# All 86 pacing waits removed from GpSimd's gathers in a field-interaction kernel with a two-layer top

## The reference, cut to what matters

```python
e = stack([tbl_f[ids[:, f]] for f in range(32)], axis=1)      # (512, 32, 16)
x = e
for W in (W0, W1, W2):                                        # (32, 32 or 64, 64)
    x = relu(einsum('bmd,bhd,mhk->bkd', e, x, W))             # e times x for all pairs (m, h)
    outs.append(x.sum(axis=2))                                # 64 features a layer
h = concat([concat(outs, 1), dense_ctx], 1)
h = relu(h @ W_top1 + b_top1); h = relu(h @ W_top2 + b_top2); y = h @ W_top3
```

## Time and profile before

| | |
|---|---|
| median of 3 runs | 333.96 us (333.34 to 334.33) |
| profiled execution | 333.23 us, of which the span from the first to the last instruction is 331.4 us |
| TensorE busy | 303.6 us of the span |
| VectorE busy | 267.0 us |
| GpSimd busy | 244.0 us, 121.8 of it 128 gathers, 121.4 of it 53 products |
| mean granted TensorE clock | 0.99 |

### The profile page before, as it was taken

One profiled execution on the slowest core, in us unless ns is written; L12 is line 12 of the kernel. 1 busy time (PEld: TensorE's weight loads), 2 busy tenths in 40 slices (PEclk: granted clock), 3 DMA queues, 4 the chain that ended last, 5 costly groups with the idle time before them and its releaser, 6 DMA issues.

```text
span 331.4 us, 4576 instructions
## 1 busy us (share of the span) xinstructions
PE 303.6 (92%) x1760; PEld 131.7 (40%) x1760; DVE 267.0 (81%) x162; ACT 65.3 (20%) x105; POOL 244.0 (74%) x187
## 2 busy tenths in 40 slices
PE   0469899999869989999999899999999999999996
PEld 0335535654436233333333233344434434434334
DVE  0118399676978999999999999999899999999110
ACT  1030511435000130122122101032213032020011
POOL 5677777778888789999888799999686539966000
PEclk9997999999989999999999999999999999999999
DMA  6364848771388869687679489929979995230000
GB/s 189 95 195 138 242 107 238 206 211 21 87 267 285 292 227 297 230 269 244 203 233 318 141 251 322 323 98 266 385 316 320 313 292 130 60 85 1 0 2 0
DMA packets 32220, 65.43 MB, mean 197 GB/s; under 512 B 5702, under 2 KB 12870, under 8 KB 32198
## 3 DMA queue, kind: packets, MB, share of 16 engines
q1 hardware_dynamic: 20614, 52.28, 46.8%
q10 hardware_dynamic: 7488, 11.80, 12.3%
q0 software_dynamic: 4096, 1.06, 3.9%
HBM read 51.35 MB, written 1.71 MB: 160 GB/s over the span
## 4 chain that ended last, share of the span: by engine, by line
PE 63%; DVE 10%; issue 9%; POOL 4%; ACT 1%; ACTq 0%; DVEq 0%; POOLq 0%
PE acc L956 55%; DVE vz L746 9%; POOL gathered L674 3%; PE factor L1001 2%; PE factor L996 1%; POOL pz L691 1%; PE acc L969 1%; PE factor L911 1%; PE acc L951 1%; PE factor L926 1%; PE factor L1008 1%; DVE feats L756 1%; PE acc L1001 1%; ACT factor L792 0%; ACTq L869 0%
## 5 line engine op out<-in xcount | busy, mean ns | idle before, releaser
L746 DVE TENSOR_TENSOR vz<-fields_sb,factor 128x1024 f32<-128x1024 f32 (+3 forms) x113 | 229.0, 2076 | 32.2 <-PE factor L911 11.1
L956 PE MATMUL acc<-vz,w_sb 128*64 128x512 f32 (+1 forms) x1020 | 197.8, 525 | 6.4 <-DVE vz L746 6.0
L674 POOL DMA_INDIRECT gathered<-in_table,index x128 | 121.8, 952 | 38.1 <-issue 31.0
L691 POOL TENSOR_TENSOR pz<-fields_sb,hidden 128x1024 f32<-128x1024 f32 (+1 forms) x53 | 121.4, 2314 | 19.0 <-DMA hidden<-relu_out 15.0
L956 PEld LDWEIGHTS acc<-vz,w_sb 128*64 128x64 f32 x1020 | 78.6, 139 | 111.3 <-issue 84.1
L956 PE MATMUL acc<-pz,w_sb 128*64 128x512 f32 (+1 forms) x212 | 52.9, 583 | 2.7 <-POOL pz L691 2.7
L858 ACT ACTIVATE relu_out<-acc 128x512 f32<-128x512 f32 (+1 forms) x30 | 15.4, 514 | 111.2 <-PE acc L956 85.8
L792 ACT ACTIVATE factor<-hidden 128x1024 f32<-128x1024 f32 (+1 forms) x26 | 23.6, 914 | 64.5 <-DMA hidden<-relu_out 45.0
L956 PEld LDWEIGHTS acc<-pz,w_sb 128*64 128x64 f32 x212 | 17.1, 137 | 30.1 <-issue 25.7
L746 DVE TENSOR_TENSOR vz<-rotated,factor 128x2048 f32<-128x2048 f32 x10 | 22.4, 2279 | 0.0
L756 DVE TENSOR_REDUCE feats<-relu_out 128x32 f32<-128x512 f32 (+1 forms) x30 | 17.1, 570 | 6.4 <-ACT relu_out L858 6.4
(11 more groups left out here) (35 smaller groups left out, 52.6 us busy)
## 6 DMA issues: line engine op xcount, KB each, us to landing
fields_sb<-fields SPq DMA_DIRECT2D x48, 512.0 KB, 5.0
rotated<-fields SPq DMA_DIRECT2D x20, 512.0 KB, 6.4
hidden<-relu_out ACTq DMA_DIRECT2D x38, 256.0 KB, 5.7
fields_sb<-fields SPq DMA_DIRECT2D x32, 256.0 KB, 3.3
own<-fields SPq DMA_DIRECT2D x5, 512.0 KB, 5.9
gathered<-in_table,index POOLq DMA_INDIRECT x128, 4.1
hidden<-relu_out ACTq DMA_DIRECT2D x14, 128.0 KB, 3.9
fields<-gathered SPq DMA_DIRECT2D x5, 256.0 KB, 2.2
```

The lines of the kernel that those rows point to most:

```text
L674: nc.gpsimd.indirect_dma_start(gathered[:, pair % GRING, j, :], None, table, bass.IndirectOffsetOnAxis(ap=index[:, i:i + 1], axis=0)).then ...
L691: nc.gpsimd.tensor_tensor(pz[:, at % PRING, 0:cols], fields[s][:, t, col:col + cols], hidden_of(step, g), ALU.mult).then_inc(pz_ready, 1)
L746: nc.vector.tensor_tensor(vz[:, at:at + nt, 0:cols].rearrange("p t (a n) -> p t a n", n=half), src[:, t:t + nt, col:col + cols].rearrange( ...
L956: last = nc.tensor.matmul(acc_of(step, ab), weights[:, kt, :], z[:, ab * half:(ab + 1) * half], start=start and j == 0, stop=stop and j == ...
```

## The change

Three tables are emptied, nothing else is changed. Gather 8 no longer waits for gather 7's landing, no gather waits for a count of TensorE's units, and none for the first spread. The order of instructions on every engine, the gathers themselves and the waits for a free place in the ring `gathered` stay.

```diff
-PACED = {12: 1, 14: 1, 15: 1, 16: 1, 17: 1, 19: 1, 20: 1, 22: 1, 24: 1, 25: 1, 26: 1, 32: 1, 34: 1, 35: 1, 36:
...
-    48, 117: 49, 118: 49, 119: 49, 120: 52, 121: 56, 123: 68, 124: 74, 125: 75, 126: 79}
-
-
-BEHIND_SPREAD = {15: 1, 41: 1, 59: 1, 75: 1, 81: 1}
-
-AFTER_ROW = (8,)
+PACED = {}
+
+
+BEHIND_SPREAD = {}
+
+AFTER_ROW = ()
```

## The result

The changed kernel takes 331.41 us in the median of six runs (331.36 to 331.55). The kernel before takes 333.21 us: six runs, 332.87 to 334.33, the three that the forecast had and three more beside the changed kernel (332.87, 332.95 and 333.09). The medians differ by 1.8 us, 0.54%. The ratio of all runs is 0.9935, 95% interval 0.9918 to 0.9951, which is a gain of 1.6 to 2.7 us. Forecast were 332.1 us, a gain of 1.9 us, the forecast's own range of 331.7 to 332.6 us and the 8-in-10 range of 331.1 to 333.8 us.

A forecast was written before the change was run, and what follows sets the result against it. GpSimd's lateness was taken to bound it, through TensorE's stall at 97 us with no slack behind. 0 + 1.35 + 0.42 + 0.1 = 1.9 us off 333.96 gave 332.1 us; own range 331.7 to 332.6, 8-in-10 range 331.1 to 333.8.

The forecast's parts named there:

- the base of the sum: Starting time of the forecast: 333.96 us, the median of the runs before, 0.73 us above its profiled execution of 333.23.
- 84 passed waits at nothing: On GpSimd's gathers: removing 84 waits that had passed already gains 0 us, 0.8 us at most.
- Gather 8 and gather 15, 1.77 us: GpSimd's gaps ahead of these gathers shrink to 0.30 us: 1.35 and 0.42 us, together 1.77 us earlier.
- The head at 0.1 to 0.2 us: At the start, descriptors of gathers 8 and 9 share DMA engines with the first loads: a slip of 0.1 to 0.2 us.
- a slip below 0.9 us costs nothing: VectorE and TensorE win 2.8 us by 103 us but can use 1.9, so a head slip up to 0.9 us is hidden.
- Full clock behind a shorter stall: Near 97 us, TensorE's stall falls from 2.65 to 0.9 us and its clock stays full: 2.8 us won, not 1.77.
- The second gate at 1.9 us: GpSimd's fifth product of (1, 6), near 204 us, lets TensorE lead by at most 1.77 + 0.1 us slack = 1.9 us.
- Behind it there is no slack: After TensorE's stall at 97 us, VectorE then TensorE are busy, so time won reaches the end unless something else is late.
- first gate: GpSimd's third product of (1, 3), for which TensorE stood 2.65 us until 96.84 us; the stall was to fall to 0.9 us.
- The larger gain (331.2 us): Rival: the product at 204 us is no limit or GpSimd's later gaps shrink; the whole 2.8 us stays; chance 0.10.
- A stretch of low clock behind the new stalls: Rival: a 0.9 us stall at 203 or 94 us lowers TensorE's clock, losing 1.7 us: 333.8 us; nothing-left class, chance 0.18.
- Gather 8 did not hold gather 7: Slower rival: gather 8 delays block 0's rows and the head, at most 4.1 us, giving 335.3 us; chance 0.09.

The follow-up runs named there:

- fourth run: Kernel before without gather 8's wait and the five waits for the first spread, the 80 waits for TensorE's counts kept: 331.6 us.
- fifth run: Kernel before with all 86 waits, gathers 68 and 69 moved behind the third product of (1, 3): 333.57 us.
- sixth run: Changed kernel with gathers 120 to 122 moved from before the last products of (1, 6) to behind the first of (1, 7): 331.03 us.
- seventh: Kernel before with all 86 waits, gathers 68 and 69 moved behind the third product of (1, 3), 120 to 122 behind the last of (1, 6): 333.09 us.
- first run: Kernel before with only gather 8's wait for gather 7's rows removed: 333.12 us.
- second run: Kernel before with only the five waits for the first spread removed: 332.62 us.
- ninth run: Changed kernel with the sixth run's gather moves, and SP writing block 1's rows only after block 0's last tile has landed: 331.31 us.

## Why the gain came out as forecast, and the time did not

- **The step that failed: the base of the sum.** The forecast took 1.9 us from 333.96 us, the median of three runs, because that median was 0.73 us above the profiled execution. The 0.73 us were chance. Six runs have a median of 333.21 us, and the 35, 23 and 11 runs beside the later kernels 333.21, 333.27 and 333.32 us, within 0.1 us of the profiled execution (333.23). So the time came out at 331.41 us, 0.7 us below the 332.1 of the sum and below the forecast's own range of 331.7 to 332.6 us. Taken from the profiled execution, as the text also did, the sum gives 331.3 us, within 0.1 of the result.
- **84 passed waits at nothing: right.** No gather's gap became shorter where a wait had passed. Gather 12's wait would have been late by 0.5 us had it stayed (fourth run); this came free with the change.
- **Gather 8 and gather 15, 1.77 us: right.** Measured 1.73 us at 93.77 us. The 0.42 us of gather 15 belong to the one profile that they were read from: with the same waits it lost 0 and 0.19 us in two others.
- **The head at 0.1 to 0.2 us: too small.** It slipped by 0.85 us in the profiled execution. Some 0.3 us of it is a late tile, and the rest, some 0.6 us near 40 us, is open: over the profiles of the other runs (the fifth apart, whose head was 2.8 us late) the row at 42.05 us began between 41.11 and 41.78 us, without order by the waits that they keep. That a slip below 0.9 us costs nothing held: it used up the whole 0.9 us stall forecast at 94 us, so TensorE's row there has none. At 0.85 us that was close.
- **Full clock behind a shorter stall: right.** In the changed kernel there was no stall left to test it (1.00 in the stretch where 0.52 stood); the fourth run's wait of 0.97 us is the test. TensorE was forecast 2.8 us earlier at 103 us and was 2.62 us ahead at 184 us, since the head had taken its part.
- **The second gate at 1.9 us: the mechanism right, the number by two errors that cancel.** The slack at the fifth product of (1, 6) was not 0.1 but nearly 0.3 us (TensorE 1.84 to 1.87 us earlier behind a product that ended 1.61 us earlier), and GpSimd had moved by 1.61, not 1.77 us, by then. The stall forecast at up to 0.9 us near 202.7 us was 0.53 us at 202.86. The three profiles that pass this gate show that it set their time. That it set the size of the gain against the first gate rests on the fourth run above all; the fifth, sixth and seventh agree with it within their noise.
- **Not in the prediction: a tile near 206 us.** "Behind it there is no slack" left out VectorE's unit that starts at 206.79 us. In the changed kernel it waited 1.35 us for its tile (to 205.61 us) and this cost nothing, since TensorE's lead stayed 1.87 us. In the first and the second run it cost TensorE 0.87 and 0.56 us.
- **The rivals.** The larger gain (331.2 us) needs the gate at 204 us to be none; it was one, and opening it in the sixth run gave 0.4 us more in the median. A stretch of low clock behind the new stalls did not come. Gather 8 did not hold gather 7: TensorE's first sums and SP's first `scratch` (14.90 us) began on time.

## What to carry to other kernels

A wait whose gap is that of its neighbours is worth nothing taken away alone, but that holds only while the engine stays as late as it is: the first run shows a gain of 1.35 us eaten by the next waits. Taking away the two named waits gave 1.6 us, taking away all 1.8. When an engine feeds another at many places, list for each place how late it is, not only the one where the consumer stands: the gain is the smallest lead over all of them, here 1.9 and not 2.8 us. Look at a wait in more than one profile: one that is just late in one execution can be in time in the next. And make the sum on a base of as many runs as there are; here the median of three was off by 0.75 us, where the effect is 1.8.

## What the runs showed of the hardware

- **A passed wait on a gather cost nothing, a late one cost the signal's delay and a little more.** The gaps are 0.30 us with none, with one and, in the fifth run, with two waits that had passed. Where gather 15 had both its waits and the spread was late for it, it started 0.77 us behind the spread's signal (24.39 - 23.62 in the kernel before, 24.44 - 23.67 in the first run, 24.00 - 23.23 in the seventh, by the semaphore events). Gather 12, with its one wait late, started 0.25 to 0.26 us behind TensorE's count (first and fourth run). So a signal that comes just as the gather before ends can still cost it 0.4 us.
- **The clock fell behind the longer stalls only.** Behind TensorE's waits of 1.89, 2.18, 2.21 and 2.65 us for the third product the next stretch was granted 0.52 to 0.66; behind waits of 0.97 and 1.33 us it was 1.00. This is the middle of the kernel, where TensorE is busy without a gap around them. In the head, behind 0.77, 0.55 and 1.42 us of waits in 7 us, the stretch from 24.7 to 28.1 us was granted 0.50 in the changed kernel and 1.00 in the ninth run, with waits of the same length.
- **The kernel before varies more.** 34 of its 35 runs beside the first four kernels reach from 332.3 to 335.4 us (one took 338.7), the six of the changed kernel from 331.36 to 331.55 us. Whether the loss of the low-clock stretch makes the difference was not tried; the sixth kernel, which has none either, spreads over 2.4 us, so it can't be all of it. The tile near 206 us is a candidate: over the profiles VectorE waited between 0 and 1.95 us for it, and the first run, with the longest wait, was the slowest of those that were profiled.
